# Packing the diagonal squares of a causal attention into five units a batch, with one key projection and the experts' biases moved

## The reference

```python
q1, k1, q2, k2, v = proj(Wq1), proj(Wk1), proj(Wq2), proj(Wk2), proj(Wv)   # 16 heads of 8
q1, k1, q2, k2 = (rotary(z) for z in (q1, k1, q2, k2))  # y1 = x1*cos + x2*sin; y2 = -x1*sin + x2*cos
s1 = einsum('bqhd,bkhd->bhqk', q1, k1)
s2 = einsum('bqhd,bkhd->bhqk', q2, k2)
pattern = where(tril, s1 / 8 * (s2 / 8), 0.0)           # causal, no softmax
y = einsum('bhqk,bkhd->bqhd', pattern, v) @ Wout.T
# gate: sigmoid scores, the best 2 of 8 experts; an expert is gelu(x @ up + up_b) @ down + down_b; a shared expert beside them
```

## Time and profile before

| | |
|---|---|
| median of 3 runs | 1614.48 us |
| the profiled execution | 1612.6 us, its span 1611.4 us |
| granted TensorE clock, mean | 0.991 |
| busy: TensorE, VectorE, ScalarE, GpSimd | 94%, 61%, 61%, 52% |
| first attention | about 51 to 519 us |
| first experts | about 519 to 770 us |

### The profile page before, as it was taken

How to read it: one execution, slowest core, us unless ns; L and a number is a source line. 1 busy time by engine, 2 the same in 40 slices (tenths; PEclk the granted TensorE clock), 3 DMA queues, 4 the chain that set the end, 5 groups by cost and what they waited for, 6 DMA issues and landing times.

```text
span 1611.4 us, 46794 instructions
## 1 busy us (share of the span) xinstructions
PE 1517.2 (94%) x18059; PEld 1107.6 (69%) x18059; DVE 981.5 (61%) x2063; ACT 986.3 (61%) x2039; POOL 831.8 (52%) x908
## 2 busy tenths in 40 slices
PE   7999999999999999999999889999998999999895
PEld 5545454555544999999778656666666999997663
DVE  6788898877776222222599968756664222225887
ACT  5766666777766555445455557677776545455773
POOL 7334488888875555555112210277764555553433
PEclk9999999999999999999999989999999999999998
DMA  9910002110002899999344320011113545532434
GB/s 314 418 66 2 7 30 78 51 32 30 30 26 36 217 247 253 253 247 240 92 118 118 85 56 3 15 48 47 47 43 55 95 91 99 93 76 80 133 108 126
DMA packets 296954, 169.45 MB, mean 105 GB/s; under 512 B 198080, under 2 KB 273216, under 8 KB 293792
## 3 DMA queue, kind: packets, MB, share of 16 engines
q1 hardware_dynamic: 246608, 128.32, 29.8%
q0 software_dynamic: 16832, 34.64, 6.3%
q10 hardware_dynamic: 33296, 3.50, 1.9%
HBM read 96.74 MB, written 69.63 MB: 103 GB/s over the span
## 4 chain that ended last, share of the span: by engine, by line
PE 63%; POOL 12%; issue 10%; DVE 7%; ACT 4%; DMA 2%; SPq 1%; POOLq 0%; DVEq 0%; ACTq 0%
PE ps L1880 14%; PE ps L1871 14%; POOL xd L630 6%; POOL s_S L663 4%; PE ps L1684 4%; PE ps L1775 4%; PE ps L1812 4%; PE ps L1912 4%; ACT s_PX L889 3%; PE ps L1900 3%; DVE s_RS L1350 3%; PE ps L1708 2%; PE ps L1822 2%; PE ps L1841 2%; PE ps L1648 2%
## 5 line engine op out<-in xcount | busy, mean ns | idle before, releaser
L630 POOL DMA_INDIRECT xd<-s_XN,s_slots x256 | 251.7, 983 | 83.9 <-issue 62.3
L823 ACT ACTIVATE s_S<-ps 128x512 f32<-128x512 f32 x384 | 208.4, 595 | 141.3 <-PE ps L1684 141.3
L1538 DVE TENSOR_TENSOR s_PP<-ps,s_S 128x1024 f32<-128x1024 f32 x192 | 234.4, 1221 | 74.1 <-PE ps L1684 52.7
L1684 PE MATMUL ps<-s_QM,s_KK 32*128 32x512 f32 x1536 | 233.8, 639 | 2.7 <-ACT s_S L823 2.7
L889 ACT ACTIVATE s_PX<-ps,s_scl 128x1024 f32<-128x1024 f32 x128 | 135.7, 1111 | 110.5 <-PE ps L1822 110.5
L904 ACT ACTIVATE s_HH<-ps,s_LG 128x256 f32<-128x256 f32 x284 | 125.2, 474 | 122.0 <-PE ps L1871 122.0
L663 POOL TENSOR_SCALAR_AFFINE_SELECT s_S<-s_S 128x1024 f32<-128x1024 f32 x128 | 140.8, 1100 | 114.0 <-ACT s_S L823 113.4
L647 POOL DMA_INDIRECT yd<-s_Y,s_to x142 | 136.2, 959 | 122.2 <-DVE s_Y L1480 97.8
L1350 DVE TENSOR_REDUCE s_RS<-ps 128x8 f32<-128x1024 f32 x128 | 150.3, 1216 | 63.3 <-PE ps L1779 63.3
L904 ACT ACTIVATE s_XN<-ps,s_b1s 128x256 f32<-128x256 f32 x256 | 113.4, 474 | 115.1 <-PE ps L1871 111.1
L647 POOL DMA_INDIRECT yd<-s_XN,s_to x128 | 122.7, 959 | 117.5 <-DVE s_XN L1480 95.6
(11 more groups left out here) (222 smaller groups left out, 2737.1 us busy)
## 6 DMA issues: line engine op xcount, KB each, us to landing
s_W<-in_ew SPq DMA_DIRECT2D x71, 576.0 KB, 4.6
s_X<-xd SPq DMA_DIRECT2D x540, 32.0 KB
xd<-s_zero SPq DMA_DIRECT2D x16, 1056.0 KB, 18.1
s_YG<-yd SPq DMA_DIRECT2D x32, 256.0 KB, 3.6
s_XN<-yd SPq DMA_DIRECT2D x32, 256.0 KB, 4.0
yd<-s_zero SPq DMA_DIRECT2D x7, 1056.0 KB, 27.9
s_XN<-in_x SPq DMA_DIRECT2D x8, 512.0 KB, 7.2
xd<-s_XN,s_slots POOLq DMA_INDIRECT x256
```

The costliest lines, as they stand in the source:

```text
L630: e.indirect_dma_start(out=xd, out_offset=bass.IndirectOffsetOnAxis(ap=m.slots[:, k, i:i + 1], axis=0), in_=m.XNp[:, i, 0:C + 1], in_offse ...
L823: e.mul(m.S1[u % 3][:, t * 512:(t + 1) * 512], m.PA[:, t * 512:(t + 1) * 512], 1.0 / 64.0).then_inc(s.ev1, 1)
L1538: e.tensor_tensor(m.PP[u % 4][:], m.PB[u % 2], m.S1[u % 3][:], ALU.mult).then_inc(s.prod, 1)
L1684: return e.matmul(out, m.KK[k][32 * r:32 * r + 32, kind, kc * P:(kc + 1) * P], m.QM[k][32 * r:32 * r + 32, kind, :, qc * P:(qc + 1) * P], ...
```

## The change

The diagonal squares of 128 are cut into squares of 64. Of a diagonal square, keys 64 to 127 against queries 0 to 63 are above the diagonal and are left out. Unit 0 of a batch (packed) holds, for all 16 heads, keys and queries 0 to 63 of both diagonal squares: even row groups go to partitions 0 to 63, odd ones to 64 to 127. Units 1 and 2 (high) hold keys 0 to 127 against queries 64 to 127 of both. Units 3 and 4 are the square across, as before. So a batch has UB = 5 units and NU is 160.

- TensorE: `scores_packed` and `scores_high` use matmuls of 256 columns, two on the same row group in turn; packed ones are 32 x 64 tiles. `weigh_packed` works on 64-partition halves with 64 columns, `weigh_high` with 64 columns, `weigh_across` as before. Key projections have one matmul in place of two.
- VectorE: for keys, the one product is read twice (with cosines and with sines); the sine half is shuffled within 32 partitions (p ^ 4), then subtracted. The table of biases goes away.
- GpSimd: `causal` covers units 0, 1 and 2, with a second select on partitions 0 to 63 for unit 0.
- SyncE: packed weighing needs the odd row groups' values on partitions 64 to 127, where the matching products lie. `moved_values` brings them by four DMAs a batch with runs of 8 values (32 bytes). For batch 0 they are issued behind the fills and two constants. The first experts' weights are loaded behind the moves of batch 10. The load of `upb` goes.
- The up biases come with each expert's weights: 4624 bytes a partition.
- The hand-written places of projections, routing, scatters (from unit 42) and waits follow the five units.

```diff
-NU = NB * 6
+UB = 5
+NU = NB * UB
-ROUTED_BY = [6, 7, 8, 9]
+ROUTED_BY = [5, 6, 7, 8]
-EW = 2 * HID + C
+EW = 2 * HID + C + 4
...
+def moved_values(e, m, s, b):
+    g = b // 2
+    e.wait_ge((s.va, s.vd)[g % 2], g // 2 + 1)
+    e.wait_ge(s.zvm, 3)
+    if b >= 1:
+        e.wait_ge(s.pv, 3 * (b - 1) + 1)
+    for h in range(4):
+        src = m.RS[0:64, b * 256:b * 256 + 256].rearrange("p (k r h d) -> p r h k d", k=4, r=2, h=4)[:, 1, h, :, :]
+        e.dma_start(m.VM[b % 2][64:128, 2, h:16:4, 8 * h:8 * h + 8], src).then_inc(s.v2, 16)
...
-    e.dma_start(m.upb[:], a["up_b"].rearrange("e (p j) -> p e j", j=4)).then_inc(s.upb, 16)
     e.dma_start(m.r0.low[:], a["c_low"].bitcast(BF16)).then_inc(s.const, 16)
     e.dma_start(m.r0.ones[:], a["c_ones"].bitcast(BF16)).then_inc(s.const, 16)
-    e.wait_ge(s.zero, 272)
-    e.wait_ge(s.zero_y, 128)
-    turn_counts(e, m, s, m.r0, 0)
-    for i in range(m.x0.NWB):
-        expert_weights(e, m, s, i)
+    for b in range(NB):
+        moved_values(e, m, s, b)
+        if b == 0:
+            e.wait_ge(s.zero, 272)
+            e.wait_ge(s.zero_y, 128)
+        if b == ROUTED_BY[0] - 1:
+            turn_counts(e, m, s, m.r0, 0)
+        if b == 10:
+            for i in range(m.x0.NWB):
+                expert_weights(e, m, s, i)
...
+    if u % UB == 0:
+        low = sel[0:64, :, :]
+        e.wait_ge(s.mask, 4 * (u // UB) + 1)
+        e.affine_select(out=low, in_=low, pattern=[[0, 16], [1, 64]], ...)
...
+        e.stream_shuffle(m.KX[:], rt[:, 256:512], [p ^ 4 for p in range(32)]).then_inc(s.kx, 1)
+        e.wait_ge(s.kx, 2 * b + x // 2 + 1)
+        e.tensor_tensor(m.KK[b % 2][:, x // 2, :], rt[:, 0:256], m.KX[:], ALU.subtract).then_inc(s.ka, 1)
...
+def scores_packed(e, m, k, kind, out, t):
+    for x in range(2):
+        for half in range(2):
+            r, at = 2 * t + half, P * x
+            i = e.matmul(out[64 * half:64 * half + 64, 256 * x:256 * x + 256], m.KK[k][32 * r:32 * r + 32, kind, at:at + 64],
+                         m.QM[k][32 * r:32 * r + 32, kind, :, at:at + 64], start=True, stop=True, skip_group_check=True)
+    return i
+def scores_high(e, m, k, kind, out, r):
+    for x in range(2):
+        i = e.matmul(out[:, 256 * x:256 * x + 256], m.KK[k][32 * r:32 * r + 32, kind, x * P:(x + 1) * P],
+                     m.QM[k][32 * r:32 * r + 32, kind, :, x * P + 64:(x + 1) * P], start=True, stop=True, skip_group_check=True)
+    return i
...
+def weigh_packed(e, m, s, b, heads):
+    e.wait_ge(s.prod, UB * b + 1)
+    e.wait_ge(s.vm, b + 1)
+    e.wait_ge(s.v2, 64 * (b + 1))
...
+    for h in heads:
+        for x in range(2):
+            for c in range(4):
+                at = 512 * (c // 2) + 256 * x + 64 * h
+                lanes = slice(64 * (c % 2), 64 * (c % 2) + 64)
+                values = m.VM[b % 2][lanes, 2, 8 * x + 4 * (c // 2) + h, :] if c % 2 else m.VM[b % 2][lanes, x, 4 * c + h, :]
+                i = e.matmul(m.PS[6][32 * c:32 * c + 32, P * x:P * x + 64], values, PP[lanes, at:at + 64], ...)
...
         if v == 0 and b + 1 < NB:
             projection(e, m, s, b + 1, 2)
+        if v == 1 and b >= 1:
+            weigh_across(e, m, s, b - 1)
+        if v == 2 and b + 1 < NB:
+            projection(e, m, s, b + 1, 3)
+        if v in (2, 3) and b < NB:
+            weigh_packed(e, m, s, b, (2 * v - 4, 2 * v - 3))
+        if v == 3 and b + 2 < NB:
+            projection(e, m, s, b + 2, 0)
+        if v == 4:
+            weigh_high(e, m, s, b)
         if v == 4 and b + 2 < NB:
-            projection(e, m, s, b + 2, 0)
+            projection(e, m, s, b + 2, 1)
```

More of the change, by code:

```diff
@@ L53, in route_step @@
 def route_step(u):
[L55 to L59, removed]
+    if u < 20:
+        return {0: 1, 1: 2, 3: 1}.get(u % UB, 0)
+    return {20: 1, 21: 1, 23: 1, 26: 2, 31: 1, 33: 1, 36: 2, 38: 1, 40: 1, 41: 1, 43: 1, 45: 1}.get(u, 0)
 def scatter_steps():
     steps, n = {}, 0
-    for u in range(56, NU):
-        for _ in range((1, 1, 2, 1, 1, 0)[u % 6]):
-            if n < 2 * NT and (n != NT or u % 6 == 0):
+    for u in range(42, NU):
+        for _ in range((1, 1, 2, 2, 0)[u % UB]):
+            if n < 2 * NT and (n != NT or u % UB == 2):
                 steps.setdefault(u, []).append((n % NT, n // NT))
@@ L245, in memory @@
     m.SC = sbx(at, "SC", [P, NT, E])
-    m.upb = sbx(at, "upb", [P, E, 4])
+    sbx(at, "empty", [P, E * 4])
     m.big = sbx(at, "big", [P, E, 72])
@@ L262, in memory @@
     m.PP = [sbx(at, f"PP{k}", [P, 1024]) for k in range(4)]
-    m.VM = [sbx(at, f"VM{k}", [P, 2, 16, 32]) for k in range(2)]
+    m.VM = [sbx(at, f"VM{k}", [P, 3, 16, 32]) for k in range(2)]
+    m.KX = sbx(at, "KX", [P, 256])
     at.close()
@@ L798, in query_masks @@
     if b >= 2:
[L799 removed]
+        e.wait_ge((s.sc1, s.sc2)[kind], (2 * UB, UB)[kind] * (b - 1))
     for j in js:
@@ L1203, in gate_first @@
     o.mark(e.tensor_tensor(m.big[:], bcast(m.tix, 1, E), bcast(base[:, 1, :], 2, 72), ALU.is_ge))
-    eid, oh = (sc[:].rearrange("p i e -> p (i e)")[:, 72 * q:72 * (q + 1)] for q in range(2))
+    eid = sc[:].rearrange("p i e -> p (i e)")[:, 0:72]
     o.wait()
@@ L1210, in gate_first @@
     o.wait()
-    o.mark(e.tensor_copy(m.idxb, eid))
+    e.tensor_copy(m.idxb, eid).then_inc(s.ub, 1)
     yield
[L1213 to L1226, removed]
 def gate_second(e, m, s, o):
@@ L1663, in values_logits, with scores_across @@
     i.then_inc(s.vl, 1)
+def scores_packed(e, m, k, kind, out, t):
[10 more added lines that the diff above has]
+    return i
+def scores_across(e, m, k, kind, out, r):
+    return e.matmul(out, m.KK[k][32 * r:32 * r + 32, kind, 0:P], m.QM[k][32 * r:32 * r + 32, kind, :, P:2 * P],
+                    start=True, stop=True)
 def score_units(e, m, s, u):
@@ L1680, in scores @@
     def scores(n, kind, t):
-        k, pair, r = (n // 6) % 2, (n % 6) // 2, 2 * (n % 2) + t
-        kc, qc = (0, 0, 1)[pair], (0, 1, 1)[pair]
+        k, v = (n // UB) % 2, n % UB
         out = (m.PB[n % 2] if kind else m.PA)[:, t * 512:(t + 1) * 512]
-        return e.matmul(out, m.KK[k][32 * r:32 * r + 32, kind, kc * P:(kc + 1) * P],
-                        m.QM[k][32 * r:32 * r + 32, kind, :, qc * P:(qc + 1) * P], start=True, stop=True)
+        if v == 0:
+            return scores_packed(e, m, k, kind, out, t)
+        if v < 3:
+            return scores_high(e, m, k, kind, out, 2 * (v - 1) + t)
+        return scores_across(e, m, k, kind, out, 2 * (v - 3) + t)
     for t in range(2):
@@ L1968, in tensor_program @@
             values_logits(e, m, s, 2 * k + q)
-    for u in range(-1, NU + 4):
-        v, b = u % 6, u // 6
+    for u in range(-1, NU + 2):
+        v, b = u % UB, u // UB
         if u < NU:
@@ L1975, in tensor_program @@
             continue
-        q, heads = pair_of(u)
-        if v == 5 and b + 2 < NB:
-            projection(e, m, s, b + 2, 1)
-        if q is not None:
-            weigh_first(e, m, s, q, heads)
         if v == 0 and b + 1 < NB:
             projection(e, m, s, b + 1, 2)
-        if v == 2 and b + 1 < NB:
-            projection(e, m, s, b + 1, 3)
-        if v == 3 and b + 2 in ROUTED_BY:
-            e.wait_ge(s.rt, 4 * (b + 1) + 4)
-            stage = ROUTED_BY.index(b + 2)
+        if v == 1 and b >= 1:
+            weigh_across(e, m, s, b - 1)
+        if v == 1 and b + 1 in ROUTED_BY:
+            e.wait_ge(s.rt, 4 * (b + 1) + 3)
+            stage = ROUTED_BY.index(b + 1)
             if stage == 0:
```

127 lines of the change are left out of this document (70 added, 57 removed).

## The result

1878.95 us, the median of four runs (1874.32 to 1890.90), against 1613.36 of the kernel before measured beside it: 1.166 times as long, with an interval of 1.159 to 1.172. The prediction was 1776, its range ended at 1805. The side was right and the size was not.

What follows compares the result with a forecast made beforehand. TensorE, without free time in the first attention, was taken as the bound. Batches +131, stall +28 and clock +2.3 made +161 on 1612.6, 1774, or 1776 as median; own range 1750 to 1800, widened to 1620 to 1805.

Steps and rivals of the forecast that it cites:

- Key projection 0.63, weighing 0.57 and 1.01 a piece: TensorE, first attention: two key projections a batch fall from 1.06 to 0.63 us; weighing stays at 3.17 us a batch.
- Mixed step 4.2, batch 18.4: First attention: four score pieces of two shapes run one after another, 4.2 us instead of 1.07, twice a batch; batch 18.4.
- Rival A: Mixed steps: shapes run together at 1.9 us, batch 13.8, the stall remains, result 1630 us; chance 15%.
- Rival B: Mixed steps and packed weighing: halves of a packed piece exclude each other, +4.4 us a batch, result 1915 us; chance 7%.
- 131 for 32 batches: First attention: each batch 4.1 us longer than 14.24, over 32 batches less one step at the end, +131 us.
- Stall 28, ending at 89: Before batch 0's packed weighing: TensorE waits from about 61 to 89 us for moved values behind fills, +28 us (26 to 34).
- The clock: +2.3, 0 to 5.: TensorE restarting after the stall's long rest: its first passes run slower, +2.3 us, range 0 to 5.
- VectorE, ScalarE and GpSimd cost nothing: First attention: these engines stay under TensorE's 18.4 us a batch, GpSimd highest at about 13.1 us; cost nothing.
- The bias sums: VectorE: removing them empties slots that were not on the path; worth nothing.
- Slower by 161: Whole kernel: 131 for the batches, 28 for the stall, 2.3 for the clock, added to 1612.6 us; slower had chance 0.93.

Runs made afterwards that it cites:

- f4: Changed kernel with mixed-step pieces ordered packed, packed, full, full, and batch 0's values moved ahead of the fills: 1633.64 us, 1.014 times the kernel before.
- f3: Changed kernel with each matmul of the mixed steps over all 128 rows instead of 32, output not the reference's: 1759.19 us, 1.091 times the kernel before.
- f1_before: The kernel before, unedited, run on the second set's chip: 1611.23 us, 1.000.
- f2: The changed kernel, unedited, run on the second set's chip: 1883.54 us, 1.169 times the kernel before.
- g1: Kernel before with only the keys projected once, VectorE shuffling the sine half: 1613.79 us, 1.001 times the kernel before.
- g3: Changed kernel with same-shape pieces issued together and ScalarE issuing the moves of batches 0 to 2: 1624.75 us, 1.007 times the kernel before.
- g2_bias: Kernel before with only the up biases loaded with each expert's weights and VectorE's bias table removed: 1609.13 us, 0.998 times the kernel before.
- the first set: Four earlier experiments, edits of the changed kernel or the kernel before, on another chip, where the kernel before took 1673.22 us.
- e3: Kernel before with only the keys projected once, on the slower chip: 1676.39 us, 1.003 times the kernel before there.
- e1: Changed kernel with only the order of mixed-step pieces changed, same shapes together, on the slower chip: 1852.15 us, 1.107 times the kernel before there.

## Why the prediction was wrong

- **Key projection 0.63, weighing 0.57 and 1.01 a piece**: measured 0.63, 0.58, and 1.03 (high) and 1.01 (across). Right; 64 columns were no risk on the chip of the forecast.
- **Mixed step 4.2, batch 18.4**: measured 4.12 and 18.26. Right, and for the reason given: f4 changed the order of the pieces (and one DMA at the start), and the step fell to 2.09. Rival A fell, since pieces of two shapes never lie side by side. Rival B fell too, since eight packed passes on two row groups take 1.01 and not 1.9.
- **131 for 32 batches**: f3, nearly all at full clock, has a stage 144.4 us longer than f1_before's, 27.8 of it the stall. That leaves 117, not 131. The forecast took 14.24 us for every batch of before, but 9 of the first 16 took 15.0 to 15.6 there. f3's, behind the stall, took 18.2 to 18.5, but for one of 21.7 and a last of 17.3.
- **Stall 28, ending at 89**: right at full clock, as f3's 27.80 shows. In the profile after it ended at 88.7 but was 22.1 long, as TensorE came 5 us later than in f3: the stage began 2.0 later, and its way to the wait took 14.3 us and not 11.1, by its own half clock.
- **The clock: +2.3, 0 to 5.** This is the step that failed. The term priced TensorE's restart after the stall and took the granted clock of the earlier trace rows, 1.00, for the rest, since TensorE would stay busy. It did stay busy, and the clock fell to half inside and after the mixed steps. The size is 124 us (f2 against f3). With it the sum would be 131 + 22 + 124 = 277, against 270 measured. Without it, in f3, the kernel took 148 us more than before, near the 161 forecast.
- **VectorE, ScalarE and GpSimd cost nothing**: right for this kernel, which idles them. It fails as soon as TensorE is quick: g1's copies come late by 0.34 us a batch more than before's (0.20, 0.38 and 0.16, less 2 x 0.20), while GpSimd's part in f4 stays open. The bias sums, priced at nothing, were worth about 4 us.
- **"Slower by 161"** split as 131 of shapes, 28 of stall. With both mended (g3) the packed kernel is still 0.7% slower than before, with a stage as long as that of g2_bias, which has no packing (465.3 and 465.1): in these orders packing the squares gave nothing, since it saves one step and doubles two others.

The Trainium skill, TensorEngine Tiling (Array Packing), Key Properties, says that a change of tiling mode drains the engine; the trace agrees, at 4.12 us for four pieces and 2.09 for two groups. Its Gotcha 1, that different row tiles cannot use one bank at a time, is not borne out: both halves of a packed piece write one bank and run in 1.01.

## What to carry to other kernels

A tile of few rows costs its columns whatever it leaves empty, so count for each step how many row groups work at the same time, and put pieces of one shape next to each other. A profile that shows an engine 100% busy says nothing of its clock: read the granted clock of each stretch too, and treat a step in which part of the array rests as one that may halve it. Before pricing a removed operation at nothing because its engine has room, look for the stretch in which that engine is late; here that was worth more (about 4 us) than the packing.

## What the runs showed of the hardware

- TensorE's clock fell to half at 374.0 us with no rest before it in the rows, in a mixed step on 32-row tiles, and came back at about 391. With the same passes on 128 rows (f3) it stayed full behind the stall, but for 3.4 us. Whether it is the rows at work, or what they compute, these runs don't tell apart.
- At half clock a packed piece goes from 1.01 to 1.90 us. f2_after's stage has 310.6 us at half, f3_dense's 34.1; it is 123 us longer.
- Two packed pieces on four row groups, sixteen passes, run in 1.03 us (306.29 to 307.32); one, of eight passes on two row groups, takes 1.01.
- Small DMAs behind or between fills are slow to issue as well as to land: two moves of values took ScalarE's issuing side 10.22 us (g3), and in the kernel after the moves issued from 68.89 on let TensorE go on only at 88.70.
- On the first set's chip the kernel before was 3.7% slower (1673.22 against 1613.36). Weight loads waited for their issue there: in the second attention of e3 those of the weighing with 64 columns for 39.9 us, against 4.4 in the trace of the kernel before; in e1 TensorE's own are 0.44 to 1.12 us each. Their cause was not looked for and stays open.
